# A quarter of the columns of the softmax denominators' additions moves from VectorE to GpSimd

## The reference, cut to what matters

```python
x = ln(x + L0_attn(x))            # linear attention, 16 heads
x = ln(x + L0_xattn(x, ctx))      # softmax cross-attention, 8 heads of 64
x = ln(x + L0_ffn(x))             # 64 experts, 8 per token, and a shared one
x = ln(x + L1_attn(x))            # softmax over 1024 tokens
x = ln(x + L1_xattn(x, ctx))      # ternary weights; two softmax passes over the context
x = ln(x + L1_ffn(x))
```

## Time and profile before

| engine | busy us | share of the span |
|---|---|---|
| PE (matmul) | 1603.8 | 84% |
| DVE | 1373.2 | 72% |
| ACT | 1133.3 | 59% |
| POOL | 166.7 | 9% |

### The profile page before, as it was taken

How to read it: one execution, slowest core, us unless ns; L and a number is a source line. 1 busy time by engine, 2 the same in 40 slices (tenths; PEclk the granted TensorE clock), 3 DMA queues, 4 the chain that set the end, 5 groups by cost and what they waited for, 6 DMA issues and landing times.

```text
span 1909.9 us, 25458 instructions
## 1 busy us (share of the span) xinstructions
PE 1603.8 (84%) x8933; PEld 573.0 (30%) x8946; DVE 1373.2 (72%) x2251; ACT 1133.3 (59%) x1529; POOL 166.7 (9%) x104
## 2 busy tenths in 40 slices
PE   3877999999999999999789864999956468978954
PEld 2411333333333333333222222434323312312313
DVE  4486888878887878878699987666633267677774
ACT  4676776757867668677356752555523446655532
POOL 6200000000000000000000003444410000000000
PEclk8757999999999999999899975999978758977977
DMA  3000000000000000000300001111100000000000
GB/s 93 6 1 4 1 1 1 1 1 7 1 1 1 1 2 1 1 1 1 76 1 1 1 1 31 42 45 41 29 1 0 1 1 1 1 0 1 1 1 22
DMA packets 11863, 20.23 MB, mean 11 GB/s; under 512 B 1558, under 2 KB 11046, under 8 KB 11558
## 3 DMA queue, kind: packets, MB, share of 16 engines
q1 hardware_dynamic: 11750, 18.76, 3.7%
HBM read 18.23 MB, written 0.52 MB: 10 GB/s over the span
## 4 chain that ended last, share of the span: by engine, by line
PE 57%; DVE 17%; issue 13%; ACT 6%; POOL 5%; DMA 2%; SPq 0%; POOLq 0%; DVEq 0%; ACTq 0%
PE PS L1620 20%; PE PS L1605 15%; PE PS L1654 4%; DVE WRK L1034 4%; POOL WRK L527 4%; DVE KNB L983 3%; PE PS L1573 3%; PE PS L1499 2%; PE PS L1491 2%; ACT WRK L662 1%; PE PS L1662 1%; DMA KNB<-in_ctx_fm_dram 1%; PE PS L1871 1%; PE PS L1483 1%; PE PS L1850 1%
## 5 line engine op out<-in xcount | busy, mean ns | idle before, releaser
L1034 DVE TENSOR_TENSOR WRK<-WRK 128x1024 f32<-128x1024 f32 x500 | 610.6, 1221 | 50.6 <-ACT WRK L662 38.2
L662 ACT ACTIVATE WRK<-PS 128x1024 f32<-128x1024 f32 (+1 forms) x510 | 511.5, 1023 | 165.4 <-PE PS L1605 125.1
L1620 PE MATMUL PS<-WRK,V 128*64 128x512 f32 (+1 forms) x2040 | 511.3, 613 | 0.0
L983 DVE CUSTOM_DVE_ANT_0 KNB<-PS,KNB 128x458 f16<-128x458 f32 (+2 forms) x464 | 333.5, 729 | 131.3 <-PE PS L1662 105.0
L681 ACT ACTIVATE KNB<-PS 128x458 f16<-128x458 f32 (+1 forms) x336 | 185.7, 553 | 93.7 <-PE PS L1654 93.0
L1749 PE MATMUL PS<-WRK,KNB 128*128 128x512 f16 x828 | 199.1, 387 | 28.6 <-DVE KNB L924 10.9
L1605 PE MATMUL PS<-Q,KB 64*128 64x512 f16 (+1 forms) x1428 | 196.0, 384 | 23.8 <-ACT WRK L662 23.0
L1620 PEld LDWEIGHTS PS<-WRK,V 128*64 128x64 f32 (+1 forms) x2040 | 119.8, 136 | 213.0 <-issue 183.3
L1605 PE MATMUL PS<-KNB,KB 64*128 64x512 f16 (+1 forms) x1224 | 154.3, 378 | 0.3 <-ACT WRK L662 0.2
L1749 PEld LDWEIGHTS PS<-WRK,KNB 128*128 128x128 f16 x828 | 78.1, 99 | 141.6 <-issue 33.3
L1605 PEld LDWEIGHTS PS<-Q,KB 64*128 64x128 f16 (+1 forms) x1428 | 65.6, 94 | 157.8 <-ACT WRK L662 66.9
(11 more groups left out here) (320 smaller groups left out, 1681.7 us busy)
## 6 DMA issues: line engine op xcount, KB each, us to landing
V<-in_moe_w_dram SPq DMA_DIRECT2D x44, 192.0 KB, 2.4
KNB<-in_ctx_fm_dram SPq DMA_DIRECT2D x1, 2401.5 KB, 17.9
CTX<-in_ctx_fm_dram SPq DMA_DIRECT2D x1, 2401.5 KB, 13.7
KNB<-in_bit_w_dram SPq DMA_DIRECT2D x1, 960.0 KB, 15.3
PWK<-in_pair_w_dram SPq DMA_DIRECT2D x4, 192.0 KB, 2.9
SM<-in_small_dram SPq DMA_DIRECT2D x1, 716.5 KB, 4.5
XT<-in_x_fm_dram SPq DMA_DIRECT2D x1, 512.0 KB, 5.4
X<-in_x_tm_dram SPq DMA_DIRECT2D x1, 512.0 KB, 7.1
```

The lines of the kernel that those rows point to most:

```text
L662: e.activation(PR[0:r, u % 2, b, :], bank(2 * b, 2 * b + 2, slice(0, r)), ACT.Exp).then_inc(S("exp"), 1)
L983: return e.tensor_tensor_reduce(diffs, sums, diffs, 0.5, NEG, ALU.add, ALU.max, accum_out=out)
L1034: e.tensor_tensor(ACC[0:r, hf % 2, :], ACC[0:r, hf % 2, :], part, ALU.add).then_inc(S("acc"), 1)
L1620: ins = e.matmul(PS[h * HD:(h + 1) * HD, 4, :], v(r, j, h), PR[0:r, unit_no(hf, i) % 2, b, h * HALF:(h + 1) * HALF], start=(j == 0), stop= ...
```

## The change

`SHARE` is 768. DVE's additions now cover columns 0 to 767, and POOL makes the same additions for columns 768 to 1023, with a semaphore of its own, `acc_pool`. The exponential of unit u and the denominators' matmul wait for both. POOL's program gets 102 additions in pair 3 and as many in each other pair and in halves 8 and 9 together; its all-reduces of pair 3 now stand between the additions, at the slots that `CHAIN` gives them, and the clearing of `BW` in slot 1 of pair 3.

```diff
+SHARE = 3 * T // 4
@@ gpsimd
-            e.wait_ge(S("pv"), unit_no(2 * PAIRS - 2, 0))
-            e.wait_ge(S("mx"), micro_base(PAIRS - 1))
-            link(e.memset(BW[:, 0:128], 0.0))
-            e.sem_inc(S("bit_zero"), 1)
-            e.wait_ge(S("bit_rows"), 1)
-            e.partition_all_reduce(BT[:, 0:7], BR[:, 0:7], P, RED.add).then_inc(S("bit_sum"), 1)
-            for i in range(3):
-                e.wait_ge(S("ax"), i + 1)
-                e.partition_all_reduce(AM[:, i:i + 1], AX[:, i:i + 1], P, RED.max).then_inc(S("am"), 1)
+            def add_up(hf, i, b):
+                n, r = tile_no(hf, i, b), rows_of(2 * i + b)
+                part = PR[0:r, unit_no(hf, i) % 2, b, SHARE:T]
+                e.wait_ge(S("exp"), n + 1)
+                if i == 0 and b == 0:
+                    if hf >= 2:
+                        e.wait_ge(S("den_ps"), hf - 1)
+                    e.tensor_copy(ACC[:, hf % 2, SHARE:T], part).then_inc(S("acc_pool"), 1)
+                else:
+                    e.wait_ge(S("acc_pool"), n)
+                    total = ACC[0:r, hf % 2, SHARE:T]
+                    e.tensor_tensor(total, total, part, ALU.add).then_inc(S("acc_pool"), 1)
+
+            def chain(x):
+                if x[0] == "bit_sums":
+                    e.wait_ge(S("bit_rows"), 1)
+                    e.partition_all_reduce(BT[:, 0:7], BR[:, 0:7], P, RED.add).then_inc(S("bit_sum"), 1)
+                elif x[0] == "max":
+                    i = x[1]
+                    e.wait_ge(S("ax"), i + 1)
+                    e.partition_all_reduce(AM[:, i:i + 1], AX[:, i:i + 1], P, RED.max).then_inc(S("am"), 1)
+
+            for p in range(PAIRS):
+                for s in range(SLOTS):
+                    before = divmod(unit_no(2 * p, s) - 1, NU)
+                    if before[0] >= 0:
+                        for b in tiles_of(before[1]):
+                            add_up(*before, b)
+                    if p + 1 == PAIRS and s == 1:
+                        e.wait_ge(S("pv"), unit_no(2 * PAIRS - 2, 0))
+                        e.wait_ge(S("mx"), micro_base(PAIRS - 1))
+                        link(e.memset(BW[:, 0:128], 0.0))
+                        e.sem_inc(S("bit_zero"), 1)
+                    if p + 1 == PAIRS:
+                        beside((CHAIN, chain), s, SLOTS)
+            add_up(2 * PAIRS - 1, NU - 1, 0)
...
-            for i in range(3, 6):
+            def whole_max(i):
                 e.wait_ge(S("ax"), i + 1)
                 e.partition_all_reduce(AM[:, i:i + 1], AX[:, i:i + 1], P, RED.max).then_inc(S("am"), 1)
+            whole_max(3)
+            for r in range(2):
+                for i in range(NU):
+                    for b in tiles_of(i):
+                        add_up(2 * PAIRS + r, i, b)
+            whole_max(4)
+            whole_max(5)
@@ scalar, exp
                     e.wait_ge(S("acc"), tile_no(hf2, i2, min(b, tiles_of(i2)[-1])) + 1)
+                    e.wait_ge(S("acc_pool"), tile_no(hf2, i2, min(b, tiles_of(i2)[-1])) + 1)
@@ vector, add_up
-                part = PR[0:r, unit_no(hf, i) % 2, b, :]
+                part = PR[0:r, unit_no(hf, i) % 2, b, 0:SHARE]
...
-                    e.tensor_copy(ACC[:, hf % 2, :], part).then_inc(S("acc"), 1)
+                    e.tensor_copy(ACC[:, hf % 2, 0:SHARE], part).then_inc(S("acc"), 1)
...
-                    e.tensor_tensor(ACC[0:r, hf % 2, :], ACC[0:r, hf % 2, :], part, ALU.add).then_inc(S("acc"), 1)
+                    total = ACC[0:r, hf % 2, 0:SHARE]
+                    e.tensor_tensor(total, total, part, ALU.add).then_inc(S("acc"), 1)
@@ tensor, denominators
                 e.wait_ge(S("acc"), (hf + 1) * KT)
+                e.wait_ge(S("acc_pool"), (hf + 1) * KT)
```

## The result

The kernel before took 1910.81 us in the median of 5 runs, the changed one 1928.04 (1924.3 to 1932.97): ratio 1.0092, 95% interval 1.0074 to 1.0111. It is slower by 17 us (0.9%), where 41 were forecast. The profiled execution has a span of 1926.3 us, 16.4 more than before.

A forecast was written before the change was run, and what follows sets the result against it. The prediction took PE to set the pace except in pair 3, where DVE does. Its terms, -7 + 18 + 29 + 1 = +41 us on 1911.6, gave 1952 us, with an 8-in-10 range of 1919 to 1976.

The forecast's parts named there:

- Changes of kind: Pair 3: POOL alternates between additions and all-reduces, about 7 us a change, making exponentials wait; +29 us, bounds 0 to +55.
- Pairs 0 to 2: First three pairs: maxima that PE waits for come somewhat earlier; -7 us, bounds -27 to +30.
- DVE's relief is hidden under PE.: In the first three pairs PE sets the pace, so DVE's shorter additions mostly save no time.
- the additions seldom meet: In the first three pairs DVE's and POOL's additions were expected to collide little, with 0.1 to 0.3 us of margin.
- Pair 3, the exclusion: DVE and POOL additions stand for each other, lengthening three kinds of slot by 25 us, part of it hidden; +18 us.
- The bound without exclusion: Pair 3: if the engines did not exclude each other, DVE's slots would gain until PE's 3.27 us decides; -14 us.
- In pair 3 DVE does: PE sets the pace except in pair 3, where DVE does, busy 48.23 of 50 us.
- The rest: Half 9's slot of 3.36 against 3.27 us gives +1 us (0 to +4); other changes of kind and the memset nothing.
- 1 (no exclusion): Rival: additions seldom meet, pair 3 gives -14 + 29, the remainder -7; 1920 us, chance 13%.
- 2 (1924): Rival: POOL's changes of kind of work are cheap or hidden while the exclusion stays; +12 us, 1924 us, chance 12%.
- The gain of 3: Rival: faster, as DVE's shorter additions speed up pair 3 until PE decides; -21 us, 1891 us, chance 8%.
- Rival 4: Collisions in the first three pairs too, or POOL's changes of kind of work near 9.9 us; 1976 us and more, chance 5%.

The follow-up runs named there:

- e2: Changed kernel with the four partition_all_reduces of pair 3 replaced by POOL copies of the same operands; 1901.91 us, ratio 0.9951.
- e7: Kernel before, with the matmul of the sums (L1654) in pairs 0 to 2 also waiting for DVE's maximum of the step before; 1915.37 us, ratio 1.0013.
- e6: Changed kernel with DVE 896 columns and POOL 128, pair 3 wholly on DVE; 1902.74 us, ratio 0.9948.
- e4: Changed kernel with copies for the all-reduces as in e2, and POOL's additions replaced by memsets that read no SBUF; 1879.26 us, ratio 0.983.
- e12: Changed kernel with bit_sums made in slot 11 right ahead of max 0, instead of in slot 10; 1916.07 us, ratio 1.0018.
- e10: Changed kernel with additions shared only in pairs 0 to 2 and the first eight units of pair 3, DVE alone elsewhere; 1892.03 us, ratio 0.9897.
- e3: Changed kernel with SHARE = 1020, so POOL adds only 4 columns; 1933.20 us, ratio 1.011.
- e8: Changed kernel with additions shared in pair 3 alone, everything else as in the kernel before; 1947.56 us, ratio 1.018.
- e9: Changed kernel with copies for the first three all-reduces of pair 3 only, max 2 in slot 43 staying an all-reduce; 1910.93 us, ratio 0.9993.
- e11: Changed kernel with DVE 640 columns, pair 3 wholly on DVE, and POOL writing its 384 columns by memset instead of adding; 1892.29 us, ratio 0.99.

## Why the prediction was right about the sign and wrong about the size

**Changes of kind: +29 forecast, 28.8 measured, the mechanism right and the size partly by luck.** Eight changes came, the first hidden as in the kernel before. The others cost 5.8 to 5.9 us toward the all-reduce and 7.35 to 7.8 back; I had put 7 on each. By halves I had 19, less 3, in half 6 and 13 in half 7: it was 14.0 (15.4 - 1.4) and 14.8 (20.2 - 5.4). The Trainium skill (GPSIMD Engine Reference, Instruction dispatch) gives approximately 6 us; the trace agrees toward the all-reduce (5.8 to 5.9) and has 7.35 to 7.8 on the way back.

The luck is in PE's clock, for which the sum had no term. In half 7 PE is busy 94.20 us in the changed kernel and 88.90 in e2 for the same 509 matmuls, at a granted clock of 0.91 and 0.97. That is 5.3 of the 14.8 us; the waits alone were about 9.5, where I had 13. PE ahead of the exponentials that wait for POOL behind max 1, and after them, and the granted clock of that stretch (0.50 is the lower of its two levels, 1.2 instead of 2.4 GHz):

```profile
1034.88 1.47 PE L1647 MATMUL PS<-Q,KB 64*128 64x512 f16 x12
1037.74 1.94 PE L1662 MATMUL PS<-WRK,V 128*64 128x512 f32 x8
1044.78 2.74 PE L1647 MATMUL PS<-Q,KB 64*128 64x512 f16 x12 [5.10 <-ACT WRK L703]
1047.45 3.58 PE L1662 MATMUL PS<-WRK,V 128*64 128x512 f32 x8
```

```profile
1044.10:1050.80 6.70, 6.02 (x20) 1.44 (x20) 5.77 (x8) 3.58 (x4) 5.98 (x6) 0.50 0.00 0
```

Such a pause costs its own length and here 2.9 us more of matmuls. In half 6 PE's busy time is no higher than in e2 (91.87 and 92.23).

**Pairs 0 to 2: -7 forecast, -18.4 measured. This step failed: "DVE's relief is hidden under PE."** I counted DVE's lateness by 12 waits of PE's weight loads and took half of it. PE's busy 20.00 of 20 us was no proof that PE set the pace: two half-height matmuls that should overlap ran one behind the other, which e7 turned into a visible wait with 2 us more of time. The 12 waits were only the visible part: the two matmuls started 25.2 us apart in all in pairs 0 to 2, 17.0 of which the change took away. e6 confirms it from the other side: the gain follows the relief in proportion, as it would not if PE's own work were the limit. These pairs moved by more than the 10 us that the prediction itself gave as a sign of being wrong. The exclusion costs little here: e4, which has none, gains 1.0 us more, and DVE's addition has a mean of 992 ns, 38 over its median. That the additions seldom meet was right: about 40 of 300 were held up.

**Pair 3, the exclusion: +18 forecast, +6.8 measured (e2). This term was mis-sized by 11 us.** The bound without exclusion was right (-14 forecast, -13.5 in e4), so the exclusion costs 20.3 us there (e2 against e4), not 32; half 7 varies by 1.6. Some of it is again the clock: PE is busy 181.1 us in pair 3 of e2 and 173.2 in e4 for the same 1010 matmuls. Two estimates in the term were too high. First, I charged DVE the whole 0.73 us of an addition on POOL. DVE's additions in e2, two slots with a round:

```profile
984.35 2.35 DVE L1076 TENSOR_TENSOR WRK<-WRK 128x768 f32<-128x768 f32 x2
...
988.48 2.35 DVE L1076 TENSOR_TENSOR WRK<-WRK 128x768 f32<-128x768 f32 x2
```

An earlier slot of this kind, instruction by instruction, with POOL's:

```profile
974.60 1.59 POOL L521 TENSOR_TENSOR WRK<-WRK 128x256 f32<-128x256 f32 x1 [1.14 <-ACT WRK L703]
974.65 0.95 DVE L1076 TENSOR_TENSOR WRK<-WRK 128x768 f32<-128x768 f32 x1
...
975.71 1.30 DVE L1076 TENSOR_TENSOR WRK<-WRK 128x768 f32<-128x768 f32 x1
976.33 1.26 POOL L521 TENSOR_TENSOR WRK<-WRK 128x256 f32<-128x256 f32 x1
976.93 1.21 DVE L1203 TENSOR_SCALAR CTX<-CTX,AI 96x1024 f32<-96x1024 f32 x1
```

The pair of additions takes 2.36 (974.65 to 977.01) instead of 2.01 (e4) and the tensor_scalar 1.21 instead of 0.74: DVE stands 0.82 us for two POOL parts, not 1.46. DVE repeats such a slot every 4.13 us (984.35 to 988.48), against 3.85 before: +0.3, where I had +1.0. The two take turns. In pair 3 of e2 all 44 of DVE's additions that were held up end 0.81 to 0.82 us after the end of POOL's, and 48 of POOL's end 0.58 to 0.59 us after the end of DVE's. So about 0.13 of DVE's 0.95 us and 0.15 of POOL's 0.73 pass beside the other's instruction, and I had counted them as standing. The Trainium skill (SBUF — State Buffer, Who interferes with whom) has the lock held for the whole instruction; these ends agree with it. Its other rule, that a tensor_reduce never contends, now has a row: L1144 takes 1213 ns in the mean before and, as L1186, 1213 in e2, where 12 of the 18 full-width ones run beside an addition on POOL.

Second, I charged every slot. Exponentials of two slots with a projection, in the kernel before and in e2:

```profile
1015.71 1.93 ACT L662 ACTIVATE WRK<-PS 128x1024 f32<-128x1024 f32 x2
...
1019.52 1.93 ACT L662 ACTIVATE WRK<-PS 128x1024 f32<-128x1024 f32 x2
```

```profile
998.68 1.93 ACT L703 ACTIVATE WRK<-PS 128x1024 f32<-128x1024 f32 x2
...
1002.49 1.93 ACT L703 ACTIVATE WRK<-PS 128x1024 f32<-128x1024 f32 x2
```

3.81 us in both: PE's 3.27 and one projection of the context (L1702, 0.60 us) decide here. From 1015.71 to 1035.64 before and 998.68 to 1018.6 in e2, five slots take 19.9 us in each kernel, with DVE busy 17.7 and 15.6 of them. The excess of e2 is in the rounds: the exponentials of the second group take 26.5 us before (1047.44 to 1073.89) and 29.5 in e2 (1030.84 to 1060.38), 1.6 of the 3.1 us more being PE's busy time for the same 147 matmuls (clock 1.00 and 0.94). "In pair 3 DVE does" (set the pace) holds for these, not for the stretch.

**The rest: +1 forecast, -0.8 measured** (start and rest of the table), within what these stretches vary anyway. Half 9 stayed at PE's pace: 50.00 of 50 us.

Together 11.4 + 11.2 + 1.8 + 0.2 = 24.6 us, the distance from +41 to +16.4. Of the rivals, 1 (no exclusion) falls with e2 against e4. The time of 2 (1924) is the nearest to the result, but its reason is wrong: the changes cost all of their 29 us. The gain of 3 appears only where POOL doesn't read (e4). Rival 4 is out: pairs 0 to 2 gained, and no change of kind in pair 3 came near 9.9 us.

Left open: why the way back to additions costs more than the way out, and how the loss of pair 3 would split between waits and clock if the clock stayed at its upper level. Neither was tried.

## What to carry to other kernels

Before work is moved to an idle engine, look at what kinds of instruction its queue will alternate between: here four excursions to an all-reduce cost 29 us; putting two of them together (e12) took 14 of these away, and staying clear of them (e10) turned a loss of 0.9% into a gain of 1%. An engine that is busy 100% of a window may still be waiting, where its instructions can overlap and don't: compare its busy time for the same instructions in two kernels. A pause of PE can cost more than its length: look at how long the matmuls behind it take. And read a stretch slot by slot: one busy share of 96% covered slots that another engine set.

## What the runs showed of the hardware

- A change of POOL's kind of work costs 5.7 to 6.2 us toward a partition_all_reduce and 6.8 to 7.8 back to a tensor_tensor (changed kernel, e3, e8, e9, e12). Between two all-reduces, of sum and of maximum, there is none (e12). Copies or memsets in the all-reduces' place need none in pair 3 (e2, e4).
- An addition of two SBUF operands on DVE that meets one of 256 columns (0.73 us) on POOL is lengthened by 0.2 to 0.5 us (median 0.34 in pair 3 of e2), a tensor_scalar by 0.47 (1.21 against 0.74). An addition is not lengthened beside a memset (median 821 ns for 640 columns in e11) or, to speak of, one of 4 columns (e3: median 1217 ns for 1020 columns). Tensor_scalars beside memsets are (e4: up to 1.09 us against 0.75).
- Two 64-row matmuls into different banks, released together, start within 0.05 us of each other and take 0.36 us together as each does alone (e7).
- Behind a pause of PE of 5.10 us the same matmuls took 2.74 and 3.58 us instead of 1.47 and 1.94, at a granted clock of 0.50 (changed kernel, 1044 to 1051 us).
